# Attention scores carried from tile to tile by differences of keys, with one VectorE reduce for the rough maxima of two heads

## What is computed

```python
q = (layernorm(x) @ Wq).reshape(B, Nq, 16, 64)      # x: 1 x 2048 x 256
k = (context @ Wk).reshape(B, Nk, 16, 64)           # context: 1 x 1601 x 192
v = (context @ Wv).reshape(B, Nk, 16, 64)
scores = einsum('bqhd,bkhd->bhqk', q, k) / sqrt(64)
attn = softmax(scores, axis=-1)
out = einsum('bhqk,bkhd->bqhd', attn, v).reshape(B, Nq, 1024)
x = x + out @ Wo + bo
```

## Time and profile before

| | us |
|---|---|
| median of 3 runs | 1538.77 (1537.75 to 1540.24) |
| the profiled execution | 1532.58 |
| its span, first to last instruction | 1530.9 |
| TensorE busy | 1397.0 |
| VectorE busy | 938.8 |
| GpSimd busy | 908.3 |
| ScalarE busy | 675.1 |
| mean granted clock of TensorE | 0.951 of full speed |

### The profile page before, as it was taken

The page is one execution under the profiler, slowest core; times in us unless marked ns, Lnnn a source line. Parts: engine busy times, 40 slices in busy tenths (PEclk is TensorE's granted clock), DMA queues, the critical chain, the costliest instruction groups (busy, mean ns, idle before and its releaser), DMA issues. The chain is left out here.

```text
span 1530.9 us, 25311 instructions
## 1 busy us (share of the span) xinstructions
PE 1397.0 (91%) x9058; PEld 889.4 (58%) x9058; DVE 938.8 (61%) x1624; ACT 675.1 (44%) x833; POOL 908.3 (59%) x439
## 2 busy tenths in 40 slices
PE   4989999999999999999999999999987822999996
PEld 3755555555555555555555555555436822999995
DVE  7566666666666666666666666667513755565562
ACT  2224444444444444444444444444443210665653
POOL 3117777767776767777667777768683302344543
PEclk7889999999999999999999999999997955999998
DMA  7430001001001100100100010010106341444422
GB/s 235 153 140 1 22 15 58 15 16 51 22 15 38 38 15 15 58 15 22 53 15 15 22 51 22 15 43 21 64 22 220 108 139 44 119 121 123 102 32 27
DMA packets 75478, 88.87 MB, mean 58 GB/s; under 512 B 10427, under 2 KB 55516, under 8 KB 75356
## 3 DMA queue, kind: packets, MB, share of 16 engines
q1 hardware_dynamic: 68572, 78.32, 15.6%
q0 software_dynamic: 6784, 8.94, 3.6%
HBM read 58.98 MB, written 27.99 MB: 57 GB/s over the span
## 5 line engine op out<-in xcount | busy, mean ns | idle before, releaser
L687 POOL TENSOR_TENSOR acc_p<-acc_p,x_in 128x1024 f32<-128x1024 f32 x224 | 565.1, 2523 | 239.9 <-ACT x_in L751 234.1
L92 DVE TENSOR_REDUCE mx_part<-ps_m 128x1 f32<-128x512 f32 x744 | 479.0, 685 | 322.4 <-PE ps_m L80 321.7
L751 ACT ACTIVATE x_in<-ps_s 128x1024 f32<-128x1024 f32 x384 | 377.6, 1024 | 311.1 <-PE ps_s L603 306.4
L615 PE MATMUL ps_o<-x_in,v 128*64 128x512 f32 x1664 | 406.9, 607 | 0.0
L615 PEld LDWEIGHTS ps_o<-x_in,v 128*64 128x64 f32 x1664 | 99.5, 136 | 181.5 <-issue 145.2
L598 PE MATMUL ps_s<-q,k 64*128 64x512 f32 x1248 | 180.6, 391 | 0.0
L603 PE MATMUL ps_s<-m_rows,ones_row 64*128 64x512 f32 x832 | 168.7, 391 | 0.0
L598 PEld LDWEIGHTS ps_s<-q,k 64*128 64x128 f32 x1248 | 120.2, 186 | 21.5
L1297 POOL DMA_INDIRECT xg<-table,idx_g x40 | 45.8, 1145 | 137.5 <-DVE idx_g L1287 127.7
L687 POOL TENSOR_TENSOR acc_p<-x_in 128x1024 f32<-128x1024 f32 x32 | 76.0, 2377 | 62.0 <-ACT x_in L751 60.5
L623 POOL TENSOR_TENSOR acc_p<-acc_p,acc_d 128x1024 f32<-128x1024 f32 x32 | 76.6, 2395 | 41.7 <-DVE acc_d L687 41.4
(11 more groups left out here) (259 smaller groups left out, 2263.8 us busy)
## 6 DMA issues: line engine op xcount, KB each, us to landing
w_in<-in_w SPq DMA_DIRECT2D x16, 1024.0 KB, 5.0
v_st<-rec_scr SPq DMA_DIRECT2D x64, 128.0 KB, 2.9
o_scr<-v_st SPq DMA_DIRECT2D x32, 256.0 KB, 2.1
v_scr<-c_in SPq DMA_DIRECT2D x13, 512.0 KB, 2.6
v<-v_scr SPq DMA_DIRECT2D x8, 832.0 KB, 5.2
ot<-o_scr SPq DMA_DIRECT2D x2, 2048.0 KB, 11.5
x_in<-in_x SPq DMA_DIRECT2D x4, 512.0 KB, 7.7
x<-in_x SPq DMA_DIRECT2D x4, 512.0 KB, 10.3
```

The source lines that it names most:

```text
L92: dve.tensor_reduce(part[:, j // S.MF, j % S.MF:j % S.MF + 1], bank[:, 0:S.MC], AX.X, ALU.max).then_inc(G.rough_used[hd], 1)
L615: last = pe.matmul(ps_o[hd * HP:hd * HP + DH, :], v[b][:, s, hd * DH:(hd + 1) * DH], probs[:, g % RING, hd * QC:(hd + 1) * QC], start=(s = ...
L687: eng.tensor_tensor(acc, other, probs[:, (u * KT + t) % RING, :], ALU.add).then_inc(done, 1)
L751: act.activation(probs[:, g % RING, :], ps_s[:, g % 2, :], ACT.Exp, bias=G.pad_bias[:, 0:1] if s == KT - 1 else 0.0, scale=SCALE).then_inc ...
```

## The change

1. *Scores by differences.* Tiles 0 and 1 of a unit are computed as before, with m_rows. The scores of tile s from 2 on are not started anew: the slot of ps_s still holds those of tile s - 2 (less the maximum), and the three products with the difference of the keys, k[s] - k[s-2], are accumulated on top. m_rows isn't needed for these 11 tiles. The keys' buffers hold k_hi, d_hi (the high half of the 1408 differences and, behind them, the low half of the first 256 keys) and d_lo.
2. *The making of the differences.* For each block of 416 keys ScalarE still copies k_hi out; VectorE copies the block in full accuracy to kw behind the last 256 keys of the block before (for block 0 it first takes the low half of 256 keys). GpSimd subtracts within kw (pool_diff), ScalarE copies the high half (act_diff), GpSimd subtracts for the low half (pool_diff_lo), and ScalarE moves the last 256 keys to the front (act_keep). Blocks 1 to 3 have 416 differences, block 0 has 160. Four tuples say where each is put: (unit, tile) for ScalarE, (unit, number of the addition) for GpSimd, whose addition 0 takes tiles 0 and 1, 2 takes tile 5, 5 takes tile 9 and 7 takes tile 11. The prologue does the same in one piece of 1408 columns.
3. *Queries in one buffer.* q_hi and q_lo have one buffer; the blocks are made in the order PROJ_BLOCKS, each after its last use, and block q3 at (0, 2) of the pair that uses it. SP loads the weights behind it.
4. *Rough maxima.* One reduce takes both heads' banks (2 x 512 columns, or 2 x 4 x 66), and TensorE's next rough product of either head waits for it.
5. The buffers are laid out anew: the prologue's w_hi of the keys lies where d_lo will be, and the preload for the output lies in k0. GpSimd's loop has two pairs in its body, as the others have.

The diff, cut to its core; lines of context are left out:

```diff
+                d = S.DIFF
+                pool.wait_ge(s_stlo, NPJ)
+                pool.tensor_tensor(kf[:, 0:d], kf[:, S.NKP - d:S.NKP], kf[:, 0:d], ALU.subtract).then_inc(s_diff, 1)
+                pool.wait_ge(s_diff, 1)
+                pool.wait_ge(s_diff_hi, 1)
+                pool.wait_ge(s_wst[0], 64)
+                pool.tensor_tensor(G.d_lo[0][:, 0:d], kf[:, 0:d], raw(G.d_hi[0][:, 0:d]), ALU.subtract).then_inc(s_diff_lo, 1)
...
-                    dve.tensor_tensor(stage(n, 1), ps[4 + n % 4][:, 0:width(n)], raw(stage(n, 0)), ALU.subtract).then_inc(s_stlo, 1)
+                    if n == 0:
+                        dve.tensor_tensor(G.d_hi[0][:, S.DIFF:S.NKP], ps[4][:, 0:2 * P], raw(G.k_hi[0][:, 0:2 * P]),
+                                          ALU.subtract).then_inc(s_first_lo, 1)
+                        dve.wait_ge(s_first_lo, 1)
+                    if n < NPJ:
+                        dve.tensor_copy(stage(n, 1), ps[4 + n % 4][:, 0:width(n)]).then_inc(s_stlo, 1)
+                    else:
+                        dve.tensor_tensor(stage(n, 1), ps[4 + n % 4][:, 0:width(n)], raw(stage(n, 0)), ALU.subtract).then_inc(s_stlo, 1)
...
+                    if kt == 2:
+                        act.wait_ge(s_diff, 1)
+                        act.activation(G.d_hi[0][:, 0:S.DIFF], kf[:, 0:S.DIFF], ACT.Copy).then_inc(s_diff_hi, 1)
...
+PROJ_BLOCKS = (("q", 3), ("k", 0), ("q", 0), ("k", 1), ("k", 2), ("k", 3), ("q", 1), ("q", 2))
+DIFF_POOL = ((1, 0), (1, 5), (2, 0), (2, 5))
+DIFF_HI = ((1, 4), (1, 10), (2, 4), (2, 12))
+DIFF_LO = ((1, 2), (1, 7), (2, 2), (3, 0))
+DIFF_KEEP = ((1, 8), (2, 0), (2, 8))
...
-        G.q_lo.append(sb("q_lo1", [P, S.NT], F32R)[:])
-        k_hi, k_lo, q_hi, q_lo = G.k_hi, G.k_lo, G.q_hi, G.q_lo
+        k1 = sb("k1", [P, 3, S.NKP], F32R)
+        kw = sb("kw", [P, 2 * P + KC])
+        for n, x in enumerate((G.k_hi, G.d_hi, G.d_lo)):
+            x.append(k1[:, n, :])
+        k_hi, d_hi, d_lo, q_hi, q_lo = G.k_hi, G.d_hi, G.d_lo, G.q_hi, G.q_lo
...
-                wait_for(pe, rough_used[hd], count)
+                wait_for(pe, rough_used[0], count)
...
-                rough_max(S, G, dve, ps_m[:, hd, :], hd, j)
+            part = G.mx_part[:].rearrange("p (h t) c -> p h t c", h=2)
+            if j < MJOBS - 1:
+                dve.tensor_reduce(part[:, :, j // S.MF, j % S.MF], ps_m[:, :, 0:S.MC], AX.X, ALU.max).then_inc(rough_used[0], 1)
+            else:
+                dve.tensor_reduce(part[:, :, :, S.MF], ps_m[:, :, 0:S.QT * S.MT].rearrange("p h (t k) -> p h t k", k=S.MT), AX.X,
+                                  ALU.max).then_inc(rough_used[0], 1)
-            for hd in range(2):
-                dve.wait_ge(rough_used[hd], (unit + 1) * MJOBS)
+            dve.wait_ge(rough_used[0], (unit + 1) * MJOBS)
+            dve.wait_ge(rough_used[1], MJOBS)
...
+        def proj_here(n, first, last):
+            return not first if n == 0 else not last
+        def proj_count(p, n):
+            return PROJ_JOBS * p + n - 1
-            return n >= UNITS, n % UNITS
+            kind, c = PROJ_BLOCKS[n]
+            return kind == "q", c
-            if n == 0:
+            if n == 1:
...
-        def stage(n, b):
+        def act_proj(act, n, b, count):
-            w = QC if is_q else KC
-            return w, [x[b][:, c * w:(c + 1) * w] for x in ((q_hi, q_lo) if is_q else (k_hi, k_lo))]
-        def act_proj(act, n, b, count):
-            w, (hi, lo) = stage(n, b)
-            act.activation(hi, ps_x[:, 0:w], ACT.Copy).then_inc(stage_hi, 1)
-        def dve_proj(dve, n, b, count):
-            w, (hi, lo) = stage(n, b)
+            if is_q:
+                act.activation(q_hi[:, c * QC:(c + 1) * QC], ps_x[:], ACT.Copy).then_inc(stage_hi, 1)
+            else:
+                act.activation(k_hi[b][:, c * KC:(c + 1) * KC], ps_x[:, 0:KC], ACT.Copy).then_inc(stage_hi, 1)
+        def dve_proj(dve, n, b, count, p):
+            is_q, c = block_of(n)
-            dve.tensor_tensor(lo, ps_x[:, 0:w], raw(hi), ALU.subtract).then_inc(stage_lo, 1)
+            if is_q:
+                cols = slice(c * QC, (c + 1) * QC)
+                dve.tensor_tensor(q_lo[:, cols], ps_x[:], raw(q_hi[:, cols]), ALU.subtract).then_inc(stage_lo, 1)
+                return
+            if c == 0:
+                dve.tensor_tensor(d_hi[b][:, S.DIFF:S.NKP], ps_x[:, 0:2 * P], raw(k_hi[b][:, 0:2 * P]), ALU.subtract).then_inc(first_lo, 1)
+                dve.wait_ge(first_lo, p + 1)
+            else:
+                dve.wait_ge(tail_kept, (UNITS - 1) * p + c)
+            dve.tensor_copy(kw[:, 2 * P:2 * P + KC], ps_x[:, 0:KC]).then_inc(stage_lo, 1)
+        def diff_cols(c):
+            first = 0 if c else 2 * P
+            return slice(first, KC), slice(c * KC + first - 2 * P, (c + 1) * KC - 2 * P)
+        def pool_diff(pool, c, p):
+            cols, _ = diff_cols(c)
+            pool.wait_ge(stage_lo, proj_count(p, PROJ_BLOCKS.index(("k", c))) + 1)
+            pool.tensor_tensor(kw[:, cols], kw[:, cols.start + 2 * P:cols.stop + 2 * P], kw[:, cols], ALU.subtract).then_inc(diff_done, 1)
+        def act_diff(act, c, b, p):
+            cols, to = diff_cols(c)
+            act.wait_ge(diff_done, UNITS * p + c + 1)
+            act.activation(d_hi[b][:, to], kw[:, cols], ACT.Copy).then_inc(diff_hi_done, 1)
+        def pool_diff_lo(pool, c, b, p):
+            cols, to = diff_cols(c)
+            pool.wait_ge(diff_hi_done, UNITS * p + c + 1)
+            pool.tensor_tensor(d_lo[b][:, to], kw[:, cols], raw(d_hi[b][:, to]), ALU.subtract).then_inc(diff_lo_done, 1)
+        def act_keep(act, c, p):
+            act.wait_ge(diff_lo_done, UNITS * p + c + 1)
+            act.activation(kw[:, 0:2 * P], kw[:, KC:KC + 2 * P], ACT.Copy).then_inc(tail_kept, 1)
...
-            keys, qs = slice(s * P, (s + 1) * P), slice(u * QC, (u + 1) * QC)
-            for n, (k, q) in enumerate(((k_hi, q_hi), (k_lo, q_hi), (k_hi, q_lo))):
+            qs = slice(u * QC, (u + 1) * QC)
+            if s < 2:
+                keys = slice(s * P, (s + 1) * P)
+                hi, lo = k_hi[b][:, keys], d_hi[b][:, S.DIFF + s * P:S.DIFF + (s + 1) * P]
+            else:
+                keys = slice((s - 2) * P, (s - 1) * P)
+                hi, lo = d_hi[b][:, keys], d_lo[b][:, keys]
+            for n, (k, q) in enumerate(((hi, q_hi), (lo, q_hi), (hi, q_lo))):
-                    pe.matmul(ps_s[:, g % 2, hd * QC:(hd + 1) * QC], k[b][r, keys], q[b][r, qs], start=(n == 0), stop=False)
+                    last = pe.matmul(ps_s[:, g % 2, hd * QC:(hd + 1) * QC], k[r, :], q[r, qs], start=(s < 2 and n == 0), stop=(s >= 2 and n == 2),
+                                     skip_group_check=(s >= 2))
+                    if s >= 2 and n == 2:
+                        last.then_inc(scores_ready, 1)
+            if s >= 2:
+                return
...
+                    c = (u + ahead) % UNITS
+                    n = {("q", 0): PROJ_BLOCKS.index(("k", 2))}.get(("q", c), PROJ_BLOCKS.index(("q", c)))
+                    made = p if other or n == 0 else p - 1
-                        pe.wait_ge(stage_lo, PROJ_JOBS * (p if other else p - 1) + UNITS + 1 + (u + ahead) % UNITS)
+                        pe.wait_ge(stage_lo, proj_count(made, n) + 1)
+                    if j == S.MF - 1 and c == 0 and other:
+                        pe.wait_ge(stage_lo, proj_count(made, PROJ_BLOCKS.index(("k", 3))) + 1)
+                if g == 0 and not first:
+                    pe.wait_ge(first_lo, p)
+                if g == 2 and not first:
+                    pe.wait_ge(diff_lo_done, UNITS * p)
...
-                if (u, s) in PROJ_PLACES and not last:
+                if (u, s) in DIFF_KEEP and not last:
+                    act_keep(act, DIFF_KEEP.index((u, s)), p)
+                if (u, s) in PROJ_PLACES and proj_here(PROJ_PLACES.index((u, s)), first, last):
-                    act_proj(act, n, 1 - b, PROJ_JOBS * p + n)
+                    act_proj(act, n, 1 - b, proj_count(p, n))
+                if (u, s) in DIFF_HI and not last:
+                    act_diff(act, DIFF_HI.index((u, s)), 1 - b, p)
...
+                    if (u, k) in DIFF_POOL and not last:
+                        pool_diff(pool, DIFF_POOL.index((u, k)), p)
+                    if (u, k) in DIFF_LO and not last:
+                        pool_diff_lo(pool, DIFF_LO.index((u, k)), 1 - b, p)
...
-            if not last:
-                wait_for(sp, proj_ready, PROJ_JOBS * p)
-                sp_load_w(sp, p + 1)
+                wait_for(sp, proj_ready, PROJ_JOBS * p)
+                sp_load_w(sp, p + 1)
```

More of the change, by code:

```diff
@@ L79, in rough_scores @@
         t, k0 = q0 + (j // S.MF) * P, (j % S.MF) * S.MC
[L80 removed]
+        last = pe.matmul(bank[:, 0:S.MC], G.q_hi[rows, t:t + P], G.k_hi[b][rows, k0:k0 + S.MC], start=True, stop=True)
     else:
         for i in range(S.QT):
[L83 removed]
+            last = pe.matmul(bank[:, i * S.MT:(i + 1) * S.MT], G.q_hi[rows, q0 + i * P:q0 + (i + 1) * P],
```

(17 more changed lines are left out.)

27 lines of the change are left out of this document (14 added, 13 removed).

## The result

The kernel after takes 1512.9 us (median of 4 runs, 1509.2 to 1516.9) where the kernel before took 1538.3 us beside it: ratio 0.984, 95% interval 0.981 to 0.988. The profiled execution took 1513.4 us where before's took 1532.6. The forecast for the median was 1502: the range of 1472 to 1519 holds the result and the sign is right, but a third of the gain is missing, and the forecast's own range, 1490 to 1512, ends 0.9 us short of it.

A forecast was written before the change was run, and what follows sets the result against it. TensorE, busy for 91% of the span, was taken to bound the kernel. -81.4 + 27.5 + 14 + 3.5 = -36.4 us took the profiled 1532.6 to 1496.2, so 1502 for the median; range 1472 to 1519, own range 1490 to 1512.

The forecast's parts named there:

- TensorE, -81.4: In the attention, 352 pairs of ones_row and m_rows products dropped at 0.231 us each: 81.4 us less.
- The hand-over, +27.5: Between a group's rough products, the merged reduce makes TensorE lose 0.18 us, 153 times: 27.5 us more.
- GpSimd, +14: Around tile 11's addition, differences delay VectorE's addition and reduce: 14 x 0.89 = 12.5 us, plus 1.5 at block k2.
- ScalarE, SP, 0: In the attention, ScalarE's copies and waits for GpSimd, and SP's later weight loads, stay hidden: nothing.
- Ends, +3.5: Prologue 0.5 us, rough products at the attention's start 1.0, TensorE's wait for GpSimd's last sum about 2: 3.5 us.
- rival 2: In the attention, ScalarE's waits for GpSimd reach TensorE: +14 us, 1516; chance 0.20.
- What would show it: Signs: 704 instructions fewer, reduce 1.22 us, about 150 waits of 0.1 to 0.2 us, unit 32.2 to 30.6 us.
- 1 (hidden hand-over): At the hand-over, a shorter reduce or early weights make the 27.5 us fall away: 1475; chance 0.20.
- 3 (a slow reduce over two banks): At the hand-over, the two-bank reduce runs slower than the slope; at 1.60 us the kernel takes 1560; chance 0.05.
- 4: In the attention, TensorE's work falls but another engine sets the unit's pace, nothing gained: 1539; chance 0.02.

The follow-up runs named there:

- e4: The kernel after with the reduce reading 256 of each head's 512 columns; 1459.73 us, ratio 0.9488 to before.
- e9: The kernel after with one wait for both heads, rough products evenly spaced and VectorE's addition of tiles 2 and 3 moved; 1524.97 us, ratio 0.9952 to before.
- e11: The kernel before with e9's order of products and nothing of the change; 1597.59 us, ratio 1.0425 to before.
- e3: The kernel after with both heads' rough products on one semaphore and one VectorE wait; 1502.5 us, ratio 0.9761 to before.
- e1: The kernel after with a reduce for each head again, each bank handed back by itself; 1500.97 us, ratio 0.9765 to before.
- e6: The kernel after with differences made in the first pair only and reused by later pairs; 1494.36 us, ratio 0.9813 to before.
- e7: The kernel after with VectorE's additions of tiles 12 and 7 moved to other sides of reduces; 1508.47 us, ratio 0.9902 to before.
- e2: The kernel before with only the one reduce for both heads, no differences; 1539.62 us, ratio 1.0013 to before.
- e5: The kernel after with one wait, and the second rough product placed behind head 0's half of the first values product; 1621.15 us, ratio 1.0642 to before.
- e8: The kernel after with e5's order and wait and e7's moved additions together; 1622.99 us, ratio 1.0651 to before.

## Why the prediction was right or wrong

**TensorE, -81.4: right.** 704 instructions are gone, e4 is 79 us faster than before, and e9 against e11, the change with most waits hidden, is 0.9952 / 1.0425 = 0.955 of 1597.6, 73 us.

**The hand-over, +27.5: the term that was mis-sized; it is 44.** Its mechanism stands: e4 takes it away whole. The sizes of its pieces: the reduce 1.22 forecast and 1.23 seen; TensorE 0.06 forecast and 0.04 seen; but the reduce starts 0.63 or 0.64 after rough a, not 0.53. I took 0.53 from a reduce that waits for one semaphore, and the new one waits for two in a row. e3, with one wait, has 0.57: 0.07 of the 0.11 is the second wait. What the other 0.04 is wasn't tried. So rough b is 0.19 late and not 0.09, and the next spacing is 0.10 longer, which I had from the weight load (0.09): 0.29 for 0.18. The reason given for the loss, that head 0's bank used to be free early, is wrong in its weight: e1 has it back, and the group still loses 0.24. The loss comes because the scores between two rough products shrank from 1.85 to 1.4 us while VectorE's turn stayed.

**GpSimd, +14: its own work costs 4 to 5 (e6).** Place and mechanism were right and the size was not: at s = 1, units 2 and 3 show 2.15 to 2.21 against a wanted 1.95, so 14 times 0.22, 3.1 us, where I had 14 x 0.89 = 12.5; in e6, from the second pair on, where no differences are made, these fall to 1.92 to 1.97. The timeline of after, one of the 14, r0 being 677.70:

```profile
677.70 0.50 PE L81 MATMUL ps_m<-k,q 64*128 64x512 f32 x2
...
678.43 2.37 POOL L777 TENSOR_TENSOR acc_p<-acc_p,x_in 128x1024 f32<-128x1024 f32 x1
...
679.48 2.41 DVE L777 TENSOR_TENSOR acc_d<-acc_d,x_in 128x1024 f32<-128x1024 f32 x1
...
681.81 1.21 DVE L554 TENSOR_REDUCE mx_part<-ps_m 128x2 f32<-128x1024 f32 x1
...
683.08 0.50 PE L81 MATMUL ps_m<-k,q 64*128 64x512 f32 x2
```

GpSimd's addition of tile 11 ends at r0 + 3.10 and not 3.49, VectorE's addition at 4.19 and not 4.71, the reduce at 5.32 and not 5.93: the chain is as placed and 0.4 to 0.6 us earlier than placed, and most of the lateness goes with that. The work itself was put too low, and that didn't matter: a difference of 416 columns takes 1.08 us by itself and 1.41 on average, 9.5 us a pair in all and not 6.9. (The 6.9 was not added up right either: 2 x (3 x 1.02 + 0.45) is 7.0, and the line through the rows of 512 and 1024 columns gives 1.06 for 416.)

The rest of the 9 lies in three places, by the spacings: at s = 1 of every other unit 0, 2.27 or 2.28, about 1 us; at s = 2, some 0.1 us in each unit behind a held product, about 3; and at s = 9, which I had not looked at, three units (of 30) with 2.52 or 2.53 where the others have 1.92 to 1.95, 1.8 us, and one at the end. The timeline of after, one of the three:

```profile
634.38 2.37 POOL L777 TENSOR_TENSOR acc_p<-acc_p,x_in 128x1024 f32<-128x1024 f32 x1 [0.30 <-ACT x_in L850]
634.71 3.12 DVE L777 TENSOR_TENSOR acc_d<-acc_d,x_in 128x1024 f32<-128x1024 f32 x1
...
638.12 1.23 DVE L554 TENSOR_REDUCE mx_part<-ps_m 128x2 f32<-128x1024 f32 x1 [0.19 <-DVE mx L564]
...
639.40 0.50 PE L81 MATMUL ps_m<-k,q 64*128 64x512 f32 x2 [0.64 <-DVE mx_part L554]
```

VectorE's addition of tile 7 meets GpSimd's of tile 8 and takes 3.12 us instead of 1.22; the reduce is late and TensorE stands 0.64. No difference stands there, and e6 keeps all three. e3, with one wait, has none of them (1.85 in those units; at s = 1 its units 2 and 3 are later instead, 2.26 to 2.33), so it is a matter of how the queues meet, and moving the addition doesn't pay (e7). So about half of the 9 is GpSimd's extra work and half is not; that split is argued from e6 and the spacings, no run takes the other half away alone.

**ScalarE, SP, 0: right.** ScalarE waits 2.7 us for the difference seven times, and no wait of TensorE comes of it: its weight loads wait for exponentials for 26.0 us in all and 0.3 at most, and before it was 32.0 and 0.4 (150 to 1060 us).

**Ends, +3.5: 5.9.** The first rough product starts 0.9 later (94.88 for 94.00; 0.5 forecast), but in the nine other traces with the new prologue it starts anywhere from 92.8 to 95.9, so that piece can't be told from nothing. The four rough products at the start come every 2.21 us, not 1.82, 2.3 instead of 1.0: where nothing covers the turn, its whole chain is paid. The timeline of TensorE:

```profile
96.83 0.80 PE L81 MATMUL ps_m<-k,q 64*128 64x512 f32 x2 [1.45 <-DVE mx_part L554]
99.04 0.80 PE L81 MATMUL ps_m<-k,q 64*128 64x512 f32 x2 [1.42 <-DVE mx_part L554]
```

The last wait for GpSimd is 7.96 us instead of 5.26, 2.7 (2 forecast):

```profile
1124.79 1.98 PE L719 MATMUL ps_x<-acc_p,ones 128*64 128x512 f32 x4 [7.96 <-POOL acc_p L713]
```

**The sum.** -81.4 + 44 + 9 + 5.9 = -22.5 us up to that instruction; it must come out, as the 9 is a remainder. Behind it nothing was changed, and the stretch to the end is 3.2 us longer in this profile (381.7 to 384.9). That need not be a price of the change: the same stretch is 387.6 in e2, whose scores are those of before, and 385.1 to 387.8 in e1 to e4, 371.6 to 373.5 in e5 to e8 and 379.4 to 380.7 in e9 to e11, so it differs by chip and by some 2.7 on one. Together -19.3, and the profiled executions differ by 19.1. The medians differ by 25.4, because the profiled execution of before lies 5.7 us below the median of its runs and that of after 0.5 above.

So the result lies in the range by a right mechanism with two wrong sizes that partly cancel: the hand-over was put 16.5 us too low and GpSimd's term 5 too high. The stated number nearest to 1512.9 is rival 2's 1516, and its mechanism did not occur.

**What would show it.** 704 instructions, a reduce of 1.23 us and the waits came. The unit did not: from L84 to L84 (which was L83) the one like that of 644 us takes 32.2 us (633.29 to 665.49) and not 30.6. 0.48 of that is the new order of the projections, which puts a block of queries there (s = 2: 2.96 for 2.48) and takes it out elsewhere, 0.61 is the late product at s = 9, and the rest is the hand-over's five times 0.11. The other units take 31.4 to 32.4 where they took 32.2 to 33.2, two of about 34 (before as after) and the last three aside.

**The rivals.** 1 (hidden hand-over) did not come; it takes a reduce of half the size. 2 fell with ScalarE's waits: none of them reached TensorE. 3 (a slow reduce over two banks) fell with the row of 1.23 us. 4 fell.

**A better kernel** than after is e3 or e1, each at 0.976 of before, 0.8% below after; between them nothing is told apart.

## What to carry to other kernels

When work is cut from the saturated engine, list the turns of other engines that used to fit between its instructions, and compare each with the shortened gap: here a turn of 1.9 us was free at 2.18 and cost more than half of the gain at 1.73. Cost a turn from its first semaphore to the next start, each wait counted, and measure whether the work as such or its latency is in the way before giving the engine another order. An order that evens out such gaps has to be priced by itself, on the unchanged kernel: here it cost 65 us, more than the 44 it could win.
